# Attention's score pairs first, the last part's loads spread, a third quarter on chip, and another order of transfers round the seam

## The reference

```python
x = x + L0_xattn(layernorm(x), ctx, ctx)          # softmax attention, 16 heads, per-head temperature
x = x + L0_ffn(layernorm(x))                      # activations to uint8 and weights to int8, 512 -> 2048 -> 512
x = x + L1_xattn(layernorm(x), ctx, ctx, mask)    # no softmax: (q k^T / dk) v, output projection, layernorm
x = x + tanh(((layernorm(x) @ W) @ A1) @ A2 + bias)
```

## Time and profile before

| | us |
|---|---|
| median of 3 runs | 1909.57 |
| lowest, highest | 1906.88, 1909.62 |
| the profiled execution | 1910.15 |
| its span | 1908.4 |
| TensorE busy | 1804.8 |
| VectorE busy | 1551.3 |
| ScalarE busy | 1238.6 |
| GpSimd busy | 952.3 |

### The profile page before, as it was taken

One profiled execution on the slowest core, in us unless ns is written; L12 is line 12 of the kernel. 1 busy time (PEld: TensorE's weight loads), 2 busy tenths in 40 slices (PEclk: granted clock), 3 DMA queues, 4 the chain that ended last, 5 costly groups with the idle time before them and its releaser, 6 DMA issues. The chain is left out here.

```text
span 1908.4 us, 31628 instructions
## 1 busy us (share of the span) xinstructions
PE 1804.8 (95%) x9447; PEld 1354.1 (71%) x9530; DVE 1551.3 (81%) x3607; ACT 1238.6 (65%) x3379; POOL 952.3 (50%) x1053
## 2 busy tenths in 40 slices
PE   8995899999999999999878999889999999999997
PEld 7784688888888888888744444357677667767775
DVE  6764788999988999998758888878888888888874
ACT  4562889999988999999723333256555655655543
POOL 3120356666665666666610000056676666667664
PEclk9998899999999999999988999999999999999999
DMA  8377334544454445433379999264445445444311
GB/s 286 133 239 197 72 91 113 132 120 111 112 133 117 113 112 131 118 89 97 90 272 389 371 356 357 90 234 146 155 167 184 146 167 187 143 166 165 122 50 39
DMA packets 146513, 310.73 MB, mean 163 GB/s; under 512 B 44449, under 2 KB 56737, under 8 KB 128033
## 3 DMA queue, kind: packets, MB, share of 16 engines
q1 hardware_dynamic: 146192, 308.36, 50.0%
q10 hardware_dynamic: 144, 0.26, 0.0%
HBM read 167.00 MB, written 108.00 MB: 144 GB/s over the span
## 5 line engine op out<-in xcount | busy, mean ns | idle before, releaser
L1241 POOL TENSOR_TENSOR a_pr<-a_pr,a_rcp 128x512 f32<-128x512 f32 x256 | 266.4, 1041 | 300.8 <-DVE a_rcp L1087 300.4
L1000 ACT ACTIVATE a_pr<-a_s,a_nmax 128x128 f32<-128x128 f32 x1024 | 363.9, 380 | 17.1 <-DVE a_nmax L1080 15.0
L1485 PE MATMUL f_pair<-f_room,w 128*128 128x512 bf16 x999 | 226.3, 383 | 10.5 <-DVE hmax L1712 8.0
L1000 ACT ACTIVATION_READ_ACCUMULATOR a_pr<-a_s,a_nmax 128x1 f32 x1024 | 224.2, 219 | 0.0
L1932 POOL TENSOR_TENSOR f_ring<-f_ring,f_room 128x512 f32<-128x512 f32 x64 | 82.1, 1282 | 255.1 <-DVE f_room L1873 255.1
L1712 DVE CUSTOM_DVE_ANT_0 f_hf<-f_pair,nb,sh 128x512 f32<-128x512 f32 x248 | 175.1, 748 | 39.7 <-PE f_pair L1485 26.4
L1080 DVE TENSOR_REDUCE a_nmax<-a_s 128x4 f32<-128x512 f32 x256 | 173.7, 678 | 20.0 <-PE a_s L893 19.9
L1485 PEld LDWEIGHTS f_pair<-f_room,w 128*128 128x128 bf16 x1024 | 99.7, 99 | 125.4 <-DVE hmax L1712 8.5
L1095 DVE TENSOR_TENSOR a_pTl<-a_pt,a_pTh 128x512 fp32r<-128x512 f32 x256 | 168.6, 680 | 19.3 <-ACT a_pTh L1009 18.4
L1640 ACT ACTIVATE f_room<-f_ring,f_off,f_rs 128x512 f32<-128x512 f32 x128 | 103.9, 812 | 111.1 <-POOL f_off L1923 110.2
L1917 POOL TENSOR_TENSOR f_rs<-f_rs,f_half 128x1 f32<-128x1 f32 x128 | 71.9, 562 | 190.2 <-DVE f_rs L1762 190.2
(11 more groups left out here) (389 smaller groups left out, 5151.6 us busy)
## 6 DMA issues: line engine op xcount, KB each, us to landing
hidden<-f_hf SPq DMA_DIRECT2D x58, 1024.0 KB, 6.8
f_hf<-hidden SPq DMA_DIRECT2D x58, 1024.0 KB, 5.3
xb<-x SPq DMA_DIRECT2D x16, 1024.0 KB, 5.5
a_qs<-bqreph SPq DMA_DIRECT2D x128, 128.0 KB, 2.3
a_qs<-bqrepl SPq DMA_DIRECT2D x128, 128.0 KB, 2.4
a_xr<-x SPq DMA_DIRECT2D x64, 256.0 KB, 3.7
x<-a_xr SPq DMA_DIRECT2D x64, 256.0 KB, 2.5
f_ring<-x SPq DMA_DIRECT2D x64, 256.0 KB, 4.8
```

Of the source, the lines that this page charges most:

```text
L1000: last = e.activation(pr[:, t, j, :], s_bank[t][:, j * P:j * P + P], ACT.Exp, bias=nmax[kk % 2][:, t, j:j + 1], accum_out=sums[kk % 2][:, ...
L1241: e.tensor_tensor(p, p, rcp[kk % 2][:, t, :].unsqueeze(2).to_broadcast([P, 4, KEYS]), ALU.mult).then_inc(*e_pn)
L1485: last = e.matmul(h_bank[(PAIRS * u + i) % 3][:, q, :], w1[:, k, f * P:f * P + P], xT[u % 2][:, k, :], start=k == 0, stop=k == KC - 1)
```

## The change

1. In `prepare`, the keys' transfers go out after the first w2 store instead of after the last load but one; w2's third store and the last piece of m change places with the loads of WqT and x; the last load of x goes behind all stores of wc. ScalarE takes the high part of WqT before it copies the last w2 transposes out, and VectorE's norm(1) goes behind the four low parts of x.
2. In `attend`, the first pairs are issued ahead of all steps, and the values go out two steps later, in every batch.
3. In `rest`, the loads for the last stage are issued one piece at a time by `ahead(u)`, behind the third store of groups 1 to 13.
4. A third quarter, number 6, stays on chip, in xb[0]. Its memory is also where the rounded quarters 4 and 5 go, so the order is 6, 4, 5, 7 (`ORDER`). The quarters of step 2 are handled at the usual place in the step and no longer at its end.

The diff, without what is only moved by a line:

```diff
@@ prepare, ScalarE and VectorE @@
+            weight(8, place["t"][-1])
             turned(7)
-            weight(8, place["t"][-1])
...
-                if i == 2:
-                    norm(1)
                 if i == 3:
                     for k in range(KC):
                         halve("x", k, 23 + k, [x[:, k, :] for x in v1])
+                    norm(1)
@@ prepare, SyncE @@
             send_w2(0)
+            keys()
             send_w2(1)
             load(16)
             load(17)
             load(18)
-            send_m(3)
-            send_w2(2)
+            send_m(3, range(KC))
             load(19)
             load(20)
-            keys()
+            send_w2(2)
+            send_m(3, (KC,))
             send_w2(3)
             load(21)
...
-                if i == 2:
-                    load(22)
+            load(22)
@@ attend, SyncE @@
-                o = kk - VALUE + 4
+                o = kk - VALUE + 2
...
-                e_pv.wait_ge(e, 2 * (b * TPB + kk - VALUE) + 1)
+                e_pv.wait_ge(e, 2 * (b * TPB + o - 4) + 1)
...
             def step(b, kk):
-                paired(b, kk)
+                if not first(b) or kk >= 0:
+                    paired(b, kk)
                 load(b, kk)
                 store(b, kk)
                 again(b, kk)
-                if isinstance(b, int) and b == 0 and kk == -4:
+                if first(b) and kk == VALUE - 2:
                     e_const.wait_ge(e, 0)
                 vals(b, kk)
                 keys(b, kk)
+
+            paired(0, -QUERY)
@@ rest @@
-            first = {0: (), 1: (4, 5), 2: (6, 7), 3: range(8, 9 + ahead)}
+            first = {0: (), 1: (6, 4), 2: (5, 7), 3: range(8, 9 + ahead)}
...
-        AT_HAND = {4: mraw[:, 0:KC, :], 5: ring[:, 4:8, :]}
+        AT_HAND = {4: mraw[:, 0:KC, :], 5: ring[:, 4:8, :], 6: xb[0]}
+        ORDER = {6: 4, 4: 5, 5: 6}
...
-            e_w.wait_ge(e, 5)
+            e_w.wait_ge(e, 10)
@@ rest, ScalarE and VectorE, step k @@
-                if k != 2:
-                    for n in quarters(k, 0):
-                        rounded(n)
+                for n in quarters(k, 0):
+                    rounded(n)
...
-                if k == 2:
-                    for n in quarters(k, 0):
-                        rounded(n)
@@ rest, SyncE @@
-            e.dma_start(scr["w2"][:], scr["w2_dram"]).then_inc(*e_w)
-            for h in range(2):
-                e.dma_start(f32(scr["wch"][h][:]), scr["wc"][h]).then_inc(*e_w)
...
-            matrices(0)
-            for w in range(4):
-                load(w)
-            masks(0)
+            def ahead(u):
+                if u == 1:
+                    for i, n in enumerate(("L1_xattn_ln_g", "L1_xattn_ln_b", "L1_ffn_bias")):
+                        e.dma_start(scr["rows"][:, i, :], A[n].rearrange("(a n) -> a n", a=1).to_broadcast([P, D])).then_inc(*e_w)
+                elif 2 <= u < 6:
+                    fs = slice(4 * (u - 2), 4 * (u - 1))
+                    e.dma_start(scr["w2"][:, fs, :], scr["w2_dram"][:, fs, :]).then_inc(*e_w)
+                elif u == 6:
+                    matrices(0)
+                elif 7 <= u < 11:
+                    h, c = divmod(u - 7, 2)
+                    cs = slice(2 * c, 2 * c + 2)
+                    e.dma_start(f32(scr["wch"][h][:, cs, :]), scr["wc"][h, :, cs, :]).then_inc(*e_w)
+                elif u in (11, 12):
+                    load(2 * (u - 11))
+                    load(2 * (u - 11) + 1)
+                elif u == 13:
+                    masks(0)
             for u in range(NG):
                 for s in range(4):
                     keep(u, s)
                     if s == 0:
                         tokens(u + 3)
+                    if s == 2:
+                        ahead(u)
             for k in STEPS:
-                if k == -1:
-                    hidden(6)
                 hidden(k + 8)
```

More of the change, by code:

```diff
@@ L667, in send_v, with send_m @@
                     e.dma_start(scr["v"][b, h], f32(outs[b][h][:])).then_inc(*e_send[b])
-            def send_m(b):
-                for i in range(KC + 1):
+            def send_m(b, pieces=range(KC + 1)):
+                for i in pieces:
                     n = (KC + 1) * b + i
@@ L1610, in hidden @@
                 if n not in AT_HAND:
-                    e_hf[n % HR].wait_ge(e, n // HR - (1 if n % HR > 1 else 2))
+                    e_hf[n % HR].wait_ge(e, n // HR - (1 if n % HR > 2 else 2))
                 e.activation(hbuf(n), hbuf(n), ACT.Relu, scale=col2[:, 3:4]).then_inc(*e_hr)
@@ L1669, in _ @@
                 norm(k - 2, mv3, rs3, off3, xn3, e_off3, e_t3, e_xn3)
-                if k != 2:
-                    for n in quarters(k, 1):
-                        hidden(n)
+                for n in quarters(k, 1):
+                    hidden(n)
                 if cut_of(k):
@@ L1706, in hidden @@
                 if i % 2 == 0 and n not in AT_HAND:
-                    e_keep[i // 2].wait_ge(e, u - 1 if u < NG - 1 or i // 2 > 1 else u - 2)
+                    e_keep[i // 2].wait_ge(e, u - 1 if u < NG - 1 or i // 2 > 2 else u - 2)
                 if i % 2 == 0 and n == 4:
@@ L1729, in rounded @@
                     return
-                e_hr.wait_ge(e, n - HR)
+                e_hr.wait_ge(e, ORDER.get(n, n) - HR)
                 if n % 4 == 0:
                     e_y.wait_ge(e, n - 5)
+                if n == 4:
+                    e_hq.wait_ge(e, ORDER[6] - HR)
                 q = 4 * (n % 4)
@@ L1977, in matrices @@
                 if B == 1:
-                    e_hq.wait_ge(e, 0)
+                    e_hq.wait_ge(e, ORDER[4] - HR)
                 e.dma_start(mraw[:], scr["m"][NB - 1 - B]).then_inc(*e_m)
@@ L1984, in hidden @@
                 g, q = n // 4, n % 4
-                if g == 1 or g == 2 and q < 2:
+                if g == 1 or g == 2 and q < 3:
                     e_fq.wait_ge(e, 12 + q)
@@ L1996, in load @@
                 if 4 <= w < 8:
-                    e_hq.wait_ge(e, 1)
+                    e_hq.wait_ge(e, ORDER[5] - HR)
                 e.dma_start(X[w % RING], scr["x1"][TPG * group(w // 4) + w % 4]).then_inc(*e_x[w % RING])
@@ L2019, in _ @@
             tokens(2)
-            e.dma_start(scr["w2"][:], scr["w2_dram"]).then_inc(*e_w)
-            for h in range(2):
-                e.dma_start(f32(scr["wch"][h][:]), scr["wc"][h]).then_inc(*e_w)
-            for i, n in enumerate(("L1_xattn_ln_g", "L1_xattn_ln_b", "L1_ffn_bias")):
-                e.dma_start(scr["rows"][:, i, :], A[n].rearrange("(a n) -> a n", a=1).to_broadcast([P, D])).then_inc(*e_w)
-            matrices(0)
-            for w in range(4):
-                load(w)
-            masks(0)
+            def ahead(u):
[16 more added lines that the diff above has]
+                    masks(0)
             for u in range(NG):
```

1 line of the change is left out of this document (removed).

## The result

| | before | changed |
|---|---|---|
| median, us | 1909.59 (4 runs, 1906.88 to 1912.51) | 1886.61 (4 runs, 1883.58 to 1889.36) |
| profiled execution, us | 1910.15 | 1883.58 |
| its span, us | 1908.4 | 1881.8 |

The ratio is 0.9879, 95% interval 0.9858 to 0.9900: 23.0 us less by the medians, where I had said 29.1.

The account below looks back on a forecast made before the run. TensorE, busy 95% of a 1908.4 us span, was taken to bound the kernel. Terms 4.5 + 10.2 + 1.5 + 0 + 9.0 + 4.0 = 29.2 us off 1910.15, stated as 1880.5; range 1870 to 1892.

Parts of the forecast that it names:

- rival 2: Preparation: the keys' new place costs what it saves, last w2 quarter late; 1885, up to 1888 us; chance 0.09.
- The seam, end of the preparation: Before attention: earlier WoT load and wc stores bring the last landing forward; 4.5 us gained, ends 7 and -3.
- Score pairs: Attention's opening: pairs' transfers go first, so the first score comes 4.7 us after the block opens, not 14.9; 10.2 us.
- The clock: Attention's start: with less idle time the full clock is back sooner; 1.5 us gained, ends 0 and 3.
- Attention's body: Later batches: values loaded two steps later, partly no longer sharing the queue with keys; counted 0, ends -3 and 6.
- Rival 3: Batch boundaries in attention get lighter too, the 2.45 us gap and slow clock going; 6 us more, 1874.5; chance 0.07.
- The hidden-layer stage: Late loads spread over groups 1 to 13 remove the loss at the stage's start; 9.0 us gained, upper end 10.5.
- Rival 1: Hidden-layer stage: transfers bind at 362 GB/s, 1898 us, chance 0.07; half-way at 385 GB/s, 1885.7, chance 0.10.
- Rival 4: Slower than before: mixed stores and loads get only 330 GB/s in groups 1 to 13; 1918 us; chance 0.03.
- The third quarter: Last stage's opening: quarter kept on chip and earlier roundings let the fifth tile's product start sooner; 4.0 us, ends 2 and 6.

Follow-up runs that it names:

- experiment 5: Changed kernel with the twelve key transfers moved into SyncE's wait for GpSimd, between pieces of the last block of m; 1879.93 us, ratio 0.9852.
- experiment 6: Kernel with the keys in SyncE's wait, plus ScalarE's bias-row load issued after it has opened the first query tile; 1877.91 us, ratio 0.9837.
- experiment 7: Changed kernel with the values going out two steps earlier in every batch, as in the kernel before; 1894.81 us, ratio 0.9921.
- experiment 1: Changed kernel with the preparation as in the kernel before, attention and the last part as changed; 1885.40 us, ratio 0.9877.
- experiment 4: Changed kernel with only the keys' transfers put back behind the last load but one; 1887.96 us, ratio 0.9897.
- experiment 3: Kernel before with only the late loads spread, quarters 4 and 5 alone on chip; 1898.67 us, ratio 0.9948.
- experiment 2: Kernel before with only attention's transfers changed: first pairs ahead, values two steps later; 1899.87 us, ratio 0.9958.
- experiment 8: Changed kernel with the thirteen late loads going out in groups 1 to 4 instead of 1 to 13; 1895.17 us, ratio 0.9918.
- experiment 10: Changed kernel with the twelve key transfers ahead of both w2 stores rather than between them; 1884.42 us, ratio 0.9879.
- experiment 9: Kernel before with only the third quarter kept on chip and its order of roundings; 1905.21 us, ratio 0.9984.

## Why the prediction was right, and which step was wrong

The time was inside the range, and the forecast 6.1 us too low. The time measured is that of rival 2 (1885, up to 1888), to which I had given 0.09; a range of 22 us took it in. One term had the wrong sign, 8.0 us off; the others together gave 1.2 more than counted in the traces.

**The seam, end of the preparation: wrong, +3.5 instead of -4.5.** The failed step is "the nearest row says otherwise: the transfers themselves are short, and the queue was standing before stores and quantised tiles there". It was standing, but inside an issue, by the inference above for room, and not for an event of another engine: the first key transfer then stood 6.8 us as well, and the other eleven came on top. The load of the last w2 quarter left 6.75 us later, and VectorE, quantising it, passed the delay on to its end (169.96 to 176.64). The sentence before it, a loss of some 3 if the keys delay that load by all their 8 us, was this case, priced almost exactly; I gave it 0.09 as rival 2, up to 1888. With the keys in a wait for GpSimd the whole step gives 6.5, for 4.5 counted (experiment 5), and that kernel took 1879.93 us, where I had forecast 1880.5; that the two are so close is in part luck, since other terms were off by 1 to 2 us both ways.

**Score pairs: right, 8.9 for 10.2.** The pairs took 6.0 us from T to the first score and not 4.7, since ScalarE's load of the bias row went out in the same microsecond. Without that it is 4.4 (experiment 6). That the first values go out over later steps is part of the gain: experiment 7 shows what happens otherwise.

**The clock: 1.5 counted, not shown.** The first two steps of attention, 28.4 us for 30.2, are 1.8 less in this trace. But they took 30.2 to 30.6 in experiments 1, 4 and 6, which have the new transfer times, and 28.5 in experiment 3, which has the old ones. What they follow is when the lower level ended: 6.7 to 7.5 us after the first score in the changed kernel and experiments 2, 3, 5, 8 and 10 (28.4 to 28.6 us), 9.2 to 9.9 us after it in the kernel before and experiments 1, 4 and 9 (30.2 to 30.6). Experiment 6 had its low stretch later, from 9.7 to 13.1 us (30.2). Pairs sooner did not decide which of these it was.

**Attention's body: 0 counted, nothing shown clear of scatter.** The profiled executions with the new transfer times took 728.9, 732.0, 732.3, 732.0, 734.6, 731.7, 733.9 and 735.0 us between the first and last query tile (changed kernel, then experiments 10, 2, 1, 4, 5, 6, 8), mean 732.6; those with the old ones 734.6, 733.5 and 735.0 (before, experiments 3 and 9), mean 734.4. The means differ by 1.8 us, body and clock together, but the single traces overlap (728.9 to 735.0 and 733.5 to 735.0), so even this is at the edge of scatter; at least the rest of the 5.7 in the pair of traces shown above is scatter. Probably it is also why the profiled execution is 3 us faster than the median. Rival 3 (batch boundaries lighter by 6) did not come true.

**The hidden-layer stage: right, 10.8 for 9.0.** Experiment 3 alone gave 9.5 in the trace and 9.0 in the time. VectorE waited for stores up to 1.7 us, more than the 1 us I had allowed, and landings passed the slack of 11.0, yet TensorE felt none of it. Rivals 1 and 4 are out: 413 GB/s were carried with TensorE busy, and 421 when more was asked. The Trainium skill has two figures here. The section of "DMA: Bandwidth & Descriptors" that the prediction weighed has about 358 GB/s bind; the Trainium skill's page "HBM Reference", section "Specifications (TRN2)", gives that as a core's share when both cores of a domain stream, and about 425 for a core alone. The traces of this lone core agree with the latter by their 421; no run here had a second core streaming.

**The third quarter: right, 4.4 for 4.0**, and 3.3 us (0.8 to 5.3 by its interval) in the time when alone. The mechanism was as counted: the fifth product starts 3.9 us sooner for 3.6, what is left of the wait is 1.89 us for about 2, and the low part of the next tile is late by 0.76 us for 0.6.

Sum with the measured terms, from the traces: -3.5 + 8.9 + 1.8 (body and clock, at the edge of scatter) + 10.8 + 4.4 = 22.4, against 23.0 by the medians.

## What to carry to other kernels

When a transfer is moved into a stretch in which its queue "stands", look at what it stands for. If the profile lists a wait for another engine's event, the stretch can take it: here twelve transfers of 8.6 us went into a wait of 8.9, and attention started 10.0 us sooner. If the time lies inside an issue, it may not: here the newcomer stood too, and then added its own issue time to everything behind it.

A wait that shrinks is no proof that its cause came sooner; compare when both sides of it end. And when the most urgent transfers are put first, the ones that stood ahead must be spaced out as well, and other queues' loads kept out of the same microsecond.

## What the runs showed of the hardware

- One issue of a 64 KB transfer held SyncE for 6.8 us behind a store of 512 KB and two loads of 1 MB (changed kernel); ahead of that store the twelve took 0.7 to 0.9 us each on average (experiment 10). In the profile such a stand is part of the issue and not a wait.
- A lone core moved 421 GB/s over 15 us of mixed stores and loads, with TensorE busy 14.95 of 15; asked for 482 it gave 423 at most over 15 us.
- A 256 KB load on ScalarE's queue, issued with the four transfers of the pairs, delayed their landing: 3.8 to 4.1 us after their issue with it, 2.4 to 2.5 without (experiments 5 and 6).
